# A four-layer graph stack: single splits of two tiles, later loads and bias additions, four transpositions in flight

## The reference

```
x = layernorm(x + adj @ (x W0) + b0)                            # stage 0 below
x = layernorm(x + mean over 4 heads of softmax(leaky_relu(src_i + dst_j) + adj_ij) @ (x W1))
x = layernorm(x + two graph convolutions relu([h, adj h] W + b), the second with its own residual)
x = layernorm(x + relu(D^-1/2 (adj + I) D^-1/2 x W3))
```

## Time and profile before

| | us |
|---|---|
| median of 3 runs (lowest, highest) | 681.71 (681.45, 682.27) |
| the profiled execution's own time | 682.0 |
| its span, first to last instruction | 679.9 |
| PE busy | 671.5 (99%) |
| DVE busy | 526.1 (77%) |
| ACT busy | 387.3 (57%) |
| POOL busy | 154.5 (23%) |
| mean granted TensorE clock | 0.999 |

### The profile page before, as it was taken

How to read it: one execution, slowest core, us unless ns; L and a number is a source line. 1 busy time by engine, 2 the same in 40 slices (tenths; PEclk the granted TensorE clock), 3 DMA queues, 4 the chain that set the end, 5 groups by cost and what they waited for, 6 DMA issues and landing times.

```text
span 679.9 us, 14431 instructions
## 1 busy us (share of the span) xinstructions
PE 671.5 (99%) x5334; PEld 512.3 (75%) x5334; DVE 526.1 (77%) x991; ACT 387.3 (57%) x497; POOL 154.5 (23%) x252
## 2 busy tenths in 40 slices
PE   9999999999999999999999999999999999999996
PEld 7888644888888888888888888874444468886444
DVE  6267659998989989899897998999545435874785
ACT  6486358898889898898988979643101000222000
POOL 4366437401000010000101001564021102442222
PEclk9999999999999999999999999999999999999999
DMA  8999530003003030120301203013021110221011
GB/s 339 375 414 302 92 99 31 16 31 65 1 33 62 31 62 0 39 54 31 62 0 49 44 0 63 1 40 71 16 54 24 24 25 17 40 40 32 32 54 41
DMA packets 48297, 47.65 MB, mean 70 GB/s; under 512 B 36032, under 2 KB 42368, under 8 KB 46080
## 3 DMA queue, kind: packets, MB, share of 16 engines
q1 hardware_dynamic: 45664, 39.24, 18.9%
q0 software_dynamic: 2016, 7.34, 5.8%
q10 hardware_dynamic: 576, 0.52, 0.2%
HBM read 29.23 MB, written 2.13 MB: 46 GB/s over the span
## 4 chain that ended last, share of the span: by engine, by line
PE 83%; DMA 7%; DVE 4%; SPq 2%; ACT 1%; POOL 1%; issue 1%; POOLq 0%
PE ps L732 17%; PE ps L734 16%; PE ps L733 16%; PE ps L570 16%; PE ps L560 8%; DMA arena<-in_adj 4%; PE ps L573 4%; PE ps L572 4%; DMA ring_hl<-y 2%; SPq L295 2%; PE ps L677 2%; DVE arena L1026 1%; DMA ring_hl<-rho 1%; DVE ring_a L1070 1%; POOL rstd L1199 1%; ACT adj L416 1%
## 5 line engine op out<-in xcount | busy, mean ns | idle before, releaser
L734 PE MATMUL ps<-arena,ring_hl 128*128 (+1 forms) x1024 | 279.6, 273 | 0.0
L732 PE MATMUL ps<-arena,ring_hl 128*128 (+1 forms) x1024 | 278.8, 272 | 0.1
L733 PE MATMUL ps<-arena,ring_hl 128*128 (+1 forms) x1024 | 278.6, 272 | 0.0
L1070 DVE SCALAR_TENSOR_TENSOR ring_a<-rho,gam,ring_a 128x1024 f32<-128x1024 f32 x128 | 166.4, 1300 | 18.1 <-ACT ring_a L467 18.1
L1075 DVE TENSOR_TENSOR ring_hl<-ring_a,ring_hl 128x1024 f16<-128x1024 f32 x128 | 157.3, 1229 | 4.6 <-ACT ring_hl L481 4.6
L481 ACT ACTIVATE ring_hl<-ring_a 128x1024 f16<-128x1024 f32 x128 | 135.2, 1056 | 44.3 <-PE ps L734 27.6
L467 ACT ACTIVATE ring_a<-adj,shift 128x1024 f32<-128x1024 bf16 x128 | 145.7, 1139 | 0.0
L572 PE MATMUL ps<-arena,adj 128*128 128x257 f16 (+1 forms) x512 | 112.9, 273 | 0.7 <-ACT adj L416 0.7
L573 PE MATMUL ps<-arena,adj 128*128 128x256 f16 x512 | 112.9, 273 | 0.0
L570 PE MATMUL ps<-arena,adj 128*128 128x512 f16 x496 | 111.6, 379 | 0.0
L732 PEld LDWEIGHTS ps<-arena,ring_hl 128*128 128x128 f16 x1024 | 100.0, 98 | 12.9 <-DVE arena L1026 0.5
(11 more groups left out here) (112 smaller groups left out, 580.4 us busy)
## 6 DMA issues: line engine op xcount, KB each, us to landing
arena<-in_adj SPq DMA_DIRECT2D x16, 1024.0 KB, 11.6
x<-y POOLq DMA_DIRECT2D x14, 512.0 KB, 5.4
rho<-s_scratch SPq DMA_DIRECT2D x8, 512.0 KB, 3.8
x<-in_x SPq DMA_DIRECT2D x4, 512.0 KB, 13.8
out_x<-x SPq DMA_DIRECT2D x16, 128.0 KB, 1.7
arena<-in_x_turned SPq DMA_DIRECT2D x2, 512.0 KB, 5.6
arena<-in_L_gnn_W SPq DMA_DIRECT2D x1, 1024.0 KB, 11.5
arena<-in_L_gnn_a SPq DMA_DIRECT2D x1, 1024.0 KB, 13.5
```

Source lines behind the costliest of these rows:

```text
L732: nc.tensor.matmul(acc, hi, v_hi, start=(jt == 0), stop=False)
L733: nc.tensor.matmul(ps[:, b, 0:D], hi, v_lo, start=False, stop=False)
L734: ins = nc.tensor.matmul(acc, lo, v_hi, start=False, stop=(jt == T - 1))
L1070: nc.vector.scalar_tensor_tensor(a, rho[:, q, :], gam[:, at(h, 1), jt], a, op0=ALU.max, op1=ALU.mult)\
```

## The change

- `CHUNKS`: tiles 2 and 3 are split one by one instead of as a pair, so later chunks have an index one higher. The two high parts that VectorE makes (tiles 12-13 and 14-15) stand behind its takes 4 and 6, not 3 and 5.
- Loads: SyncE loads adjacency block 13 ahead of x's last quarter, not behind it. The two biases of layer 3 are loaded by ScalarE's queue at the end of the copies of stage 0, not at the end of the first product.
- `TURNS = 4`: a transposition waits for the one four before it, not two, in all stages.
- GpSimd: for tiles 12 to 15 the bias addition stands behind `inv_std(t - 1)`, ahead of `prep_lo`, where it stood behind `prep_lo` one loop earlier.

```diff
-        CHUNKS = [(0, 1), (1, 2), (2, 4), (4, 5), (5, 6)] + [(t, t + 2) for t in range(6, T, 2)]
+        CHUNKS = [(t, t + 1) for t in range(6)] + [(t, t + 2) for t in range(6, T, 2)]
...
-            return s_tc[t % 2], 16 * ((k - 1) * T // 2 + t // 2 + 1)
+            return s_tc[t % TURNS], 16 * (((k - 1) * T + t) // TURNS + 1)
...
             load_adj(12)
+            load_adj(13)
             load_x(3)
-            for n in range(13, NL):
+            for n in range(14, NL):
                 load_adj(n)
             for t in range(T):
-                if t >= 2:
-                    sp.wait_ge(*turned(1, t - 2))
+                if t >= TURNS:
+                    sp.wait_ge(*turned(1, t - TURNS))
...
-            turned_hi(*CHUNKS[1])
-            turned_hi(*CHUNKS[2])
-            turned_after = {0: CHUNKS[3:5], 1: CHUNKS[5:6], 2: CHUNKS[6:7], 3: CHUNKS[7:8]}
+            for chunk in CHUNKS[1:4]:
+                turned_hi(*chunk)
+            turned_after = {0: CHUNKS[4:6], 1: CHUNKS[6:7], 2: CHUNKS[7:8], 3: CHUNKS[8:9]}
...
-            for n, bi in enumerate((b1_in, b2_in)):
-                act.dma_start(b12[:, n, :], bi.rearrange("(a n) -> a n", a=1).partition_broadcast(P)).then_inc(ld_b12, 16)
...
                 for step, *n in behind.get(t, []):
                     step(*n)
+            for n, bi in enumerate((b1_in, b2_in)):
+                act.dma_start(b12[:, n, :], bi.rearrange("(a n) -> a n", a=1).partition_broadcast(P)).then_inc(ld_b12, 16)
...
-            turned_lo(*CHUNKS[1])
-            turned_lo(*CHUNKS[2])
+            for chunk in CHUNKS[1:4]:
+                turned_lo(*chunk)
             casts_after = {11: 0, 15: 2}
-            turned_after = {3: 8, 5: 9}
+            turned_after = {4: 9, 6: 10}
...
             for t in range(T + 1):
                 if t < T:
                     inv_std(t, t % R)
+                if 3 * R <= t + 1 < T:
+                    add_b0(t + 1)
                 for n in (t - 2,) if t < 14 else (12, 13) if t == 14 else (t - 1,):
                     if n >= 0:
                         prep_lo(1, n, n % R, x)
-                if 2 * R <= t + 2 < T:
+                if 2 * R <= t + 2 < 3 * R:
                     add_b0(t + 2)
```

More of the change, by code:

```diff
@@ L46, in graph_stack @@
     WARM = 36
+    TURNS = 4
     FRONT = 192
@@ L168, in graph_stack @@
         s_warm = sem("s_warm")
-        s_tc = [sem(f"s_tc{i}") for i in range(2)]
+        s_tc = [sem(f"s_tc{i}") for i in range(TURNS)]
         s_accp, s_sump, s_vp = sem("s_accp"), sem("s_sump"), sem("s_vp")
@@ L296, in _ @@
                                        xg[t // BANKS][:, t % BANKS, :, :].rearrange("p q f -> p (q f)"))\
-                  .then_inc(s_tc[t % 2], 16)
+                  .then_inc(s_tc[t % TURNS], 16)
             sp.wait_ge(s_cap, 1)
@@ L326, in _ @@
                 for t in range(T):
-                    if t >= 2:
-                        sp.wait_ge(*turned(k, t - 2))
+                    if t >= TURNS:
+                        sp.wait_ge(*turned(k, t - TURNS))
                     if k == 2 and t % R == 0:
@@ L335, in _ @@
                     sp.dma_start_transpose(xt[:, t, :].rearrange("p (c i) -> p c i", c=2 * K2),
-                                           xs[:, t % R, :, :].rearrange("p q f -> p (q f)")).then_inc(s_tc[t % 2], 16)
+                                           xs[:, t % R, :, :].rearrange("p q f -> p (q f)"))\
+                      .then_inc(s_tc[t % TURNS], 16)
             def store(t, u):
@@ L987, in _ @@
                 if t == 0:
-                    turned_lo(*CHUNKS[3])
                     turned_lo(*CHUNKS[4])
+                    turned_lo(*CHUNKS[5])
                 if t in casts_after:
@@ L1182, in _ @@
             pool.wait_ge(s_nh, 3)
-            pool.wait_ge(s_lo, CHUNKS[5][0])
-            for lo, hi in CHUNKS[5:]:
+            pool.wait_ge(s_lo, CHUNKS[6][0])
+            for lo, hi in CHUNKS[6:]:
                 pool.wait_ge(s_hi, hi)
```

## The result

The changed kernel takes 682.65 us (median of 22 runs) against 681.79 for the kernel before, timed beside it (22 runs): a ratio of 1.0015 [1.0008, 1.0022]. It is slower, by about 1.0 us, which is a little less than the 0.2% that I had called the limit. The range given held the median near its low end.

The account below looks back on a forecast made before the run. TensorE, busy 671.5 of 679.9 us, was taken to bound the kernel. Gains 0.67 + 0.88 + 0.28 = 1.8 us, but the ring made it net 2.3 us slower: 684.1 us (forecast case 683.2 to 684.9, chance 0.60), range 682.5 to 687.0.

Parts of the forecast that it names:

- the 0.2% that I had called the limit: Whole kernel: about 0.2% (1.4 us) is what a measurement can tell from no change.
- the ring: Tiles 12 to 15: bn_aggr, GpSimd's two steps, addition and VectorE's first step in a loop, 4.55 us against TensorE's 3.50.
- the smaller ring: Rival, tiles 12 to 15: VectorE's steps run faster while GpSimd is still, links shrink 0.4 each, end 682.4; chance 0.10.
- it overlaps the same GpSimd work as before: Argument against faster VectorE steps: the normalisation, 0.40 to 0.78 us by what runs beside it, keeps its GpSimd neighbour.
- The start's 0.67: First product: single splits of tiles 2 and 3 keep 0.39 us, VectorE's later casts win 0.28; bounds 0 and 0.9.
- I take the whole 0.28 as won: First product: moving VectorE's first cast behind take 4 removes the whole 0.28 us lost over 84 matmuls.
- both casts land badly: Lower bound of the start's gain, 0: both casts fall behind a running GpSimd subtraction.
- 0.88 + 0.28: TensorE's wait for adjacency cast 13 near 61 us (0.88) and for transposition 14 near 84 us (0.28), both gone.
- (d): At 84.17 eight small matmuls wait for transposition 14: 0.3 us lost, won back by four transpositions in flight.
- My 2.3: Net slowdown at the first small product: 2.6 us later than before, less 0.3 saved at the transposition's wait.
- rival of a falling clock: TensorE's clock halves in the 3.9 us wait before 79.0, costing 2.4 us more: 686.5; chance 0.17.
- The signs listed: L1194 near 63, 67.5, 72, 76.5; VectorE waiting for GpSimd; first small product near 79, 4 us idle; aggregation at 16.1.

Follow-up runs that it names:

- e4: Changed kernel, but TensorE does one more half tile of values before its first small products: 681.97 us, 1.0 [0.9991, 1.0009].
- e1: Changed kernel with the bias additions of tiles 12 to 15 put back to their old place: 680.37 us, 0.9982 [0.9973, 0.9991].
- e5: Kernel before with only the single splits of tiles 2 and 3 and VectorE's two casts one take later: 681.92 us, 0.9999 [0.999, 1.0007].
- e9: Kernel before with only the moved loads and four transpositions in flight: 681.03 us, 0.9985 [0.9975, 0.9994].
- e6: Kernel before with only the loads moved (block 13 ahead of x's last quarter, biases later): 682.01 us, 0.9999 [0.999, 1.0008].
- e11: Changed kernel with the bias additions back and two transpositions in flight instead of four: 682.06 us, 1.0005 [0.9995, 1.0014].
- e3: Changed kernel with the late bias additions for tiles 14 and 15 only: 681.44 us, 0.9993 [0.9984, 1.0002].
- e8: Changed kernel with the bias additions back and VectorE's two casts back behind takes 3 and 5: 680.82 us, 0.9984 [0.9975, 0.9992].
- e10: Changed kernel with only VectorE's two casts back behind takes 3 and 5: 682.88 us, 1.0017 [1.0008, 1.0027].

## Why the prediction was right, and where its numbers were off

**Direction and mechanism: shown.** The additions close a ring between GpSimd and VectorE that does not fit into TensorE's tile, and TensorE pays at the first small product: undone, the kernel is faster than before (0.9982); done alone, slower (1.0018); done by half, between; asked for later, partly hidden. That the ring outweighs the gains is shown as well. The size was not right: the median lies below the forecast's own 683.2 to 684.9 and in the smaller ring's 681.0 to 682.9. That the range holds it is owed to its lower end at 682.5, which took in part of that rival.

**The ring's size.** From the end of bn_aggr(11) to the end of L1009 I had 17.3 us; it takes 63.81 to 79.04 = 15.2. The links on GpSimd are as counted: 1.63, 2.51, 1.63, 1.62 (1.7, 2.6, 1.7, 1.7 forecast), with the small addition at 1.08 beside L1002 once more. Those on VectorE are 67.37 - 65.44 = 1.93, 2.27, 2.27 and 1.37, not 2.3, 2.8, 2.85 and 1.62. Failed: "it overlaps the same GpSimd work as before", the reason against my rival of the smaller ring. In the kernel before, the normalisation starts 0.07 us behind a GpSimd instruction of tile 13 and ends 0.15 after it:

```profile
67.61 0.67 POOL L1205 TENSOR_TENSOR rho<-x,rho 128x256 f16<-128x256 f32 x1
67.68 0.75 DVE L796 TENSOR_SCALAR x<-total,mv,rstd 128x256 f32<-128x256 f32 x1
```

In the ring GpSimd has done its steps while VectorE waited. Only the end of the low part (65.36 + 0.67 = 66.03) still overlaps the normalisation at 65.84, which takes 0.40, and so in all four tiles. With the additions back, the view of VectorE's lines from 60 to 80 us has it at 0.75:

```profile
L799 DVE TENSOR_SCALAR x<-total,mv,rstd 128x256 f32<-128x256 f32 x6 | 4.5, 751 | 1.5 <-POOL rstd L1202 1.4
```

4 x 0.35 = 1.4 of the 1.7 us that VectorE's links are shorter. The first product L966 behind it takes 0.41 in tiles 13 and 14, not 0.61, which is most of the rest. So that rival was right in its mechanism and in its size (0.4 a link), and I had given it 0.10.

**The start's 0.67: failed** in its second step, the casts. The single splits did what I said: in e4, with the copies at 5.94, tile 2 starts at 6.87 (6.86 forecast) and the aggregation at 16.29. In the changed kernel's profile x's pieces landed late (the copies of tiles 2 and 3 at 6.51, the pair's at 5.86 before). The change does not cause this, as the same start has them at 5.52 in e1; it makes this execution long. But in e1 the aggregation starts at 17.14, not 16.14. "I take the whole 0.28 as won" is the step: the first late cast takes 1.26 us, the takes behind it come late, and TensorE waits 0.7 us in place of 0.28:

```profile
10.55 1.26 DVE L978 CAST ring_hl<-arena 128x512 f16<-128x512 f32 x1
12.29 5.01 PE L563 MATMUL ps<-w,ring_hl 128*128 128x256 f16 x42 [0.70 <-DVE arena L784]
```

Where the same cast starts 0.2 us before the end of a GpSimd subtraction it takes 0.45 (e5, at 10.56), and the aggregation starts 0.46 us earlier. My lower bound, "both casts land badly", even had the wrong floor: it was put at 0, and it is below.

**The gains as a sum: held, but for the start.** The loads and the transpositions together bring 1.0 us (e9) where 0.88 + 0.28 = 1.16 was said. All gains together are 1.2 us (680.37 against 681.61), not 1.8; the start's part is what is missing. What the sum does not say is that its terms are limits in a row: cast 13, which ends at 61.4 to 62.1, and the last transpositions at about 84.5. Each takes back what was won ahead of it (e5 by the cast; e6 and e11 by the transpositions), so that no edit alone shows a gain.

**Why the total still came out near.** The terms cancel. In the profiled execution the ring begins 63.81 - 61.68 = 2.1 us later than forecast and is 2.1 shorter, so L1009 ends at 79.04 where I had 79.0. In the median the start is not late: with before's own 62.35, the measured 15.2 end at 77.6, which is 1.2 after 76.39; less 0.3 for (d) leaves 0.9. Measured: 1.0. My 2.3 was the ring's length too much (2.1), less the 0.67 of the start that I had put into it. The cost of the ring against the best kernel, 2.3 us, is 1.7 at this place in the profiles (79.10 - 77.16 - 0.22, the start of the last matmul and its pitch taken off); the other 0.5 is not behind it: from the first small product to the end of the span both profiles have 602.9 us (682.0 - 79.10 and 678.7 - 75.84). The shortest times of the two kernels, 681.77 and 680.15, differ by 1.6. By both, the rest lies ahead of the ring, in how early the executions start their aggregation; no experiment settles why that should differ between the two.

**The chances.** Slower was right, but 0.80 on slower by over 0.2% was too much: 0.15% [0.08, 0.22] is mostly within it. The smaller ring, which gave that case, deserved more, and it holds the median.

**The clock.** TensorE waited 1.56 us and not 3.9, and its granted clock stayed at 1.00 around the wait:

```profile
78.00:80.00 2.00, 0.90 (x15) 1.00 0.24 48
```

So the rival of a falling clock was not put to the test: no run here had a wait of the length that I had expected. My argument against it, that 3.9 us are shorter than the 4.2 seen at the end, was weak. In the changed kernel's profile the last matmul ends at 676.2; the clock is 1.00 until 678, 0.50 from 680, and between them:

```profile
678.00:680.00 2.00, 0.00 (x0) 0.84 0.00 0
```

A mean of 0.84 means 0.50 for the last 0.64 us, so the clock fell at about 679.4, some 3.2 us after the last matmul: after less than the 3.9 us of idle time that I expected.

**The signs listed.** L1194 at 64.68, 69.11, 73.02 and 76.92 (63, 67.5, 72, 76.5 said), VectorE waiting for GpSimd in all four tiles, the first small product at 79.10, no wait for a cast, none at 84: as said. The idle time of 4 us and the aggregation at 16.1: not so. The time of 79.10 is this late execution's; with the start of before it would be about 77.7, not far from the 77 that I had named as the sign of being wrong.

## What to carry to other kernels

When two engines hand a tile back and forth, draw the loop of waits and compare one round of it with the pace of the engine that bounds the kernel; a step moved behind one that waits for the other engine can close such a loop although no work is added. Waits that follow one another on the bounding engine are limits before they are savings: for each, ask when the next thing awaited would be ready if the first wait were gone, and try edits that meet two such limits together, since each alone may measure as nothing. A duration read beside a busy neighbour does not hold once the neighbour has to wait.

## What the runs showed of the hardware

- VectorE's normalisation L799 (128 x 256, fp32) takes 0.40 to 0.41 us in the ring, where at most the last 0.2 us of a GpSimd instruction overlap it. It takes 0.66 to 0.78 in the kernel before, where it starts up to 0.2 us behind the start of a GpSimd addition or subtraction of 128 x 256 and ends 0.15 after its end. The GPSIMD Engine Reference of the Trainium skill (section 8, Key points) names VectorE instructions of two SBUF inputs or in a two-port mode as those that contend with GpSimd; this one has a single tensor as input, so if the rule holds it is of the second kind. The section has no size for it; here it is a factor of up to 1.9.
- The cast of 128 x 512 from fp32 to fp16 takes 0.42 to 1.42 us. It hangs on how much is left of the GpSimd subtraction that is running when it starts: in the profiles of before, after, e1, e3, e4, e5, e8, e10 and e11 the first of the two casts ends 0.27 to 0.29 us after the end of that subtraction. In the kernel with the additions back, GpSimd has three subtractions of 1.15 us each in the row below, and the cast begins at 10.55, inside the third; it ends at 11.81, 0.28 behind it.

```profile
8.09 3.44 POOL L1189 TENSOR_TENSOR ring_hl<-arena,ring_hl 128x512 f16<-128x512 f32 x3 [5.22 <-ACT ring_hl L402]
```

- The first loads do not land at the same moment in each execution: the copy of tile 2, which waits for them, starts at 5.86 in the profile of before and at 6.51 in that of after. For five kernels with the same start (after, e1, e3, e4, e11) it starts at 5.52 to 6.51 and the first aggregation at 16.29 to 18.68; the casts above have their part in this. The changed kernel's 21 runs spread over 2.3 us.
